# Delta rule: a dense product in the turns of the last unit, whose result is not read

## The chip, the cores and the metric

The kernel runs as one program on one core of a Trainium2 chip. TensorE (PE) multiplies matrices, VectorE (DVE), ScalarE (ACT) and GpSimd (POOL) work on elements, and DMA queues move data between memories. The metric is the device time of one execution in microseconds. TensorE's clock is granted by the chip: the profile writes 1.00 for 2.4 GHz and 0.50 for 1.2 GHz.

## The reference

Four transformer layers with modulated layer norms are computed in float32. The change touches the attention part of the last one, a gated delta rule over 8 sequences of 512 positions with 8 heads, keys of 128 and values of 32 elements:

```python
def step(state, inp):
    q_t, k_t, v_t, a_t, b_t = inp
    retained = jnp.einsum('bhvk,bhk->bhv', state, k_t)
    rk = retained[..., None] * k_t[:, :, None, :]
    vk = v_t[..., None] * k_t[:, :, None, :]
    state = a4 * (state - b4 * rk) + b4 * vk
    return (state, jnp.einsum('bhvk,bhk->bhv', state, q_t))
q = _l2norm(_causal_dw_conv_silu(x @ Wq, conv_q).reshape(bsz, seq_len, H, KD))
...
out = out * rms * o_norm_w * jax.nn.silu(gate)
return out.reshape(bsz, seq_len, VAL_DIM) @ Wo
```

k and v are made like q (v without the norm). After it comes one more part, the channel mix, and the store of the result.

## The kernel before

`delta_rule` cuts the work into 16 units: unit u is sequence u // 2 and one half of its heads (four). A unit has four chunks of 128 positions (NT = 4), and a chunk takes nine turns (NI = 9), so a unit takes TU = 36 turns. Within a chunk the step by step recurrence is replaced by a triangular system. Its inverse is built in blocks of 32 in the turns of `invert`: X and Y are the inverse and its transpose, F a product between them; each turn issues sixteen products of 32x32 on PE (L2194), and DVE or ACT takes the result. One chunk later, in the turns of `solve`, the system is solved: turn 0 applies the state to queries and keys (L2225, not for a unit's first chunk), turns 1, 3, 5, 7 apply the inverse (L2237) and turns 2, 4, 6 the blocks before (L2230), with DVE between each and the next; turn 8 makes the output and the new state (L2243, L2247). `make` prepares the next chunk: L2179 in turn 0 spreads the decays, L2187 in turns 3 and 6 multiplies keys with queries and keys with keys (four products of 128x128).

Around these stands a list of pieces with a turn and a place each (`pieces_at`), which `in_turn` walks in the same order on every engine. Turns of a later unit's preparation lie in the turns of the unit before: the projections of queries and keys ("taps", L2281 and L2285, five products of 128x512 to each chunk of nine turns, in turns 8, 0, 1, 2 and 3, into banks P[4] and P[5]), the sums of squares (L2293), values and gates (L2270, L2271), transposed keys (L2311). An engine issues its instructions in that order, and semaphores hold it until its inputs are there. The last unit, u = 15, has no unit behind it to prepare: after its own projections are done, at 15 turns ahead of its turn 0, P[4] and P[5] are no longer written, and its own 36 turns and the nine of the last `solve` run with what belongs to it alone. Then the unit's results are scaled (`rms`), transposed (L2319) and multiplied with Wo3 (L2324), and DVE adds them to X (L2620), which ends the stage. The channel mix begins with L2654.

In the page and the trace a float32 matmul shows as two records, so that four products are x8.

```python
if 0 <= turn < NU * TU:
    invert(u, i, *INVERT[step])
for piece in at.get((turn, 2), ()):
    prepare(*piece)
```

These four lines close a turn in `in_turn`; a piece without a place of its own has place 2, and so stands behind the turn's `solve` and `invert`.

Of the kernel before, what the change touches and what calls it, by code (L numbers as in the profile page):

```python
# [24 lines left out]
T = 512  # L25
# [88 lines left out]
def ts(i, n):  # L114
    return slice(i * n, (i + 1) * n)
# [1869 lines left out]
def delta_rule(k):  # L1985
# [3 lines left out]
    with ExitStack() as s:  # L1989
# [4 lines left out]
        hp_of = lambda u: hp2[:, u // 2 % 2]  # L1994
# [22 lines left out]
        pe, act, dve, pool, dma = k.stage("delta_start")  # L2017
# [20 lines left out]
        for n in (1,):  # L2038
            pe, act, dve, pool, dma = k.stage(f"delta_taps{n}")
# [23 lines left out]
        NI = len(INVERT)  # L2063
        NU, TU = 2 * B, NT * NI

        def pieces_at():

            at = {}  # L2070

            def put(u, turn, *piece, place=2):
                at.setdefault((TU * u + turn, place), []).append((u,) + piece)

            for turn in range(-6 * NI, NU * TU, NI):
                put(0, turn - 1, "table", 0)
            for u in range(NU):
                if u % 2 == 0:
                    for turn, x in ((-55, 1), (-54, 2), (-52, 3)):
                        put(u, turn, "norm", x)  # L2080
                for turn, piece in ((-36, ("small", 0)), (-35, ("gate", 0)), (-33, ("gate", 1)), (-30, ("gate", 2)), (-24, ("gate", 3)), (-24, ("gate", 4))):
                    put(u, turn, *piece)
                for x in range(5):
                    put(u, x - 9, "norms", x)
                for x in range(32):
                    turn = NI * (x // 8) - 50 + x % 8
                    if x % 8 == 0:
                        put(u, turn - 1, "taps", x)
                    elif x % 8 >= 4:
                        put(u, turn, "taps", x, place={8: 0, 0: 0, 1: 1}.get(turn % NI, 2))  # L2090
                for x in range(0, 8, 2):
                    for j in range(TAPS):
                        put(u, NI * (x // 2) - 50 + (0, 0, 1, 3)[j], "conv", TAPS * x + j, place=(1 if j == 0 else 2))
                for x in range(8):
                    put(u, NI * (x // 2) - 46 + 4 * (x % 2), "taps_done", x, place=(1 if x % 2 == 0 else 2))
                    put(u, NI * (x // 2) - 42 + 2 * (x % 2), "squares", x)
                for x in range(NT):
                    put(u, NI * x - 14, "values", x)
                    put(u, NI * x - 13, "values_done", x)
                    put(u, NI * x - 3, "scale", x)  # L2100
                put(u, 16, "weigh", 0)
                for x in range(NT - 1):
                    put(u, NI * x - 11, "keys", x)
                    put(u, NI * x - 10, "keys_done", x)
                for turn, x in ((9, 0), (11, 1), (12, 2), (13, 3)):
                    put(u, TU + turn, "rms", x)
                if u % 2:
                    for turn, x in ((14, 0), (15, 1), (16, 2)):
                        put(u, TU + turn, "out", x)
            return at  # L2110

        def all_units(name):
# [39 lines left out]
            tap_bank = lambda run: P[4 + run % 2]  # L2152
# [15 lines left out]
            with nc.Block() as block:  # L2168
                @block.tensor
                def _(e):  # L2170
# [79 lines left out]
                    def prepare(u, what, x):  # L2250
                        tag, g = f"u{u}", u % 2
# [14 lines left out]
                        elif what == "values":  # L2266
                            emptied(e, u, "values", x)
                            cols, b = ts(g, 128), ring_bank(u, "values", x)
                            for j in range(TAPS):
                                e.matmul(b[:, 0:128], hp_of(u)[:, j + x * C:j + x * C + C], w_v[:, j, cols], start=(j == 0), stop=(j == TAPS - 1))  # L2270
                            e.matmul(b[:, 128:256], hp_of(u)[:, 3 + x * C:3 + x * C + C], k.w["Wg3"][:, cols], start=True,  # L2271
                                     stop=True).then_inc(pe.steps, pe.did(f"{tag}values{x}"))
                        elif what == "taps":
                            run, j = x // 4, x % 4
                            c, H, b = run % 2, 4 * g + run // 2, tap_bank(run)
                            if c == 0:
                                if x == 0:
                                    e.wait_ge(dve.steps, dve.at(f"u{u - g}nh"))
                                if u or run:
                                    e.wait_ge(dve.steps, dve.at(f"{tag}conv{TAPS * run - 5}" if run else f"u{u - 1}conv27"))  # L2280
                                e.matmul(b, w_q[:, ts(H, C)], hp_of(u)[:, 3:3 + T], start=True, stop=True).then_inc(pe.steps, pe.did(f"{tag}run{run}"))  # L2281
                                return
                            if j == 0 and (u or run > 1):
                                e.wait_ge(act.steps, act.at(f"{tag}run{run - 2}" if run > 1 else f"u{u - 1}run{run + 6}"))
                            ins = e.matmul(b, w_k[:, j, ts(H, C)], hp_of(u)[:, j:j + T], start=(j == 0), stop=(j == TAPS - 1))  # L2285
                            if j == TAPS - 1:
                                ins.then_inc(pe.steps, pe.did(f"{tag}run{run}"))
                        elif what == "squares":
                            e.wait_ge(pool.steps, pool.at(f"{tag}sq{x}"))
                            if x == 0 and u:  # L2290
                                e.wait_ge(dve.steps, dve.at(f"u{u - 1}ssq"))
                            row = 4 * (x % 2) + x // 2
                            e.matmul(few[0:8, :], k.w["picks"][:, row, :], squares(x), start=(x == 0), stop=(x == 7)).then_inc(pe.steps, pe.did(f"{tag}ss{x}"))  # L2293
                        elif what == "norms" and x == 1:
                            e.wait_ge(dve.steps, dve.at(tag + "rows"))
                            for i in range(NT):
                                ins = e.matmul(few[:, ts(i, 8)], sq_rows[:, ts(i, C)], k.w["ident"][0:8, 0:8], start=True, stop=True)
                            ins.then_inc(pe.steps, pe.did(tag + "ssq"))
                        elif what == "gate" and x == 2:
                            hs = ts(g, 4)  # L2300
                            e.wait_ge(dve.steps, dve.at(tag + "g"))
                            emptied(e, u, "gate", 2)
                            b = ring_bank(u, "gate", 2)
                            e.matmul(b[:, 0:16], k.w["upto3"][:], q["g"][:, :, hs], start=True, stop=True)
                            e.matmul(b[:, 16:32], k.w["ones3"][:], q["g"][:, :, hs], start=True, stop=True).then_inc(pe.steps, pe.did(tag + "cum"))
                        elif what == "keys":
                            emptied(e, u, "keys", x)
                            e.wait_ge(act.steps, act.at(tag + "run7"))
                            b = ring_bank(u, "keys", x)
                            for h in range(4):  # L2310
                                ins = e.transpose(b[:, ts(h, C)], QK[:, 1, 4 * (u % 3) + h, ts(x, C)], k.w["ident"][:])  # L2311
                            ins.then_inc(pe.steps, pe.did(f"{tag}keys{x}"))
                        elif what == "out":
                            emptied(e, u, "out", x)
                            b = ring_bank(u, "out", x)
                            if x < 2:
                                e.wait_ge(dve.steps, dve.at(tag + "normed"))
                                for i in range(NT):
                                    ins = e.transpose(b[:, ts(i, C)], O[:, i, ts(x, 4)].rearrange("p h x -> p (h x)"), k.w["ident"][:])  # L2319
                                ins.then_inc(pe.steps, pe.did(f"{tag}oT{x}"))  # L2320
                            else:
                                e.wait_ge(act.steps, act.at(f"{tag}oT1"))
                                for half in range(2):
                                    ins = e.matmul(b, k.w["Wo3"][:, half, :], OT[:, half], start=(half == 0), stop=(half == 1))  # L2324
                                ins.then_inc(pe.steps, pe.did(tag + "att"))
# [584 lines left out]
```

## Time and profile before

| what | value |
|---|---|
| median of 3 runs | 3779.19 us (3778.6 to 3787.32) |
| the profiled execution | 3768.31 us |
| its span | 3766.5 us |
| PE busy in the span | 3335.2 us, 89% |
| DVE, ACT, POOL busy | 2340.3, 1697.2, 529.5 us |
| mean granted clock | 0.916 |

The span is the time between the first and the last instruction in the trace, and the execution's own time is a little longer. The last unit's turns lie near 3584 to 3678 us of the span, the channel mix behind 3693. All positions in the trace below are us from the span's start.

### The profile page before, as it was taken

How to read it: one execution, taken by the hardware profiler on the slowest of the kernel's cores; microseconds unless marked ns; L12 is line 12 of the kernel's file. 1: busy time of each engine (PE TensorE's matmuls, PEld its weight loads, DVE VectorE, ACT ScalarE, POOL GpSimd, SP SyncE). 2: the span in 40 equal slices, each digit the busy share in tenths (PEclk: the TensorE clock that was granted, in tenths of full speed). 3: DMA queues.
4: the chain of work that ended last, by engine and by line, in shares of the span. 5: the costliest groups of instructions: out<-in, count | busy, mean ns of one | idle time of the engine just before them, and what ended most of it. 6: DMA issues, size and time to landing. Idle time of an engine off the chain costs nothing. (4 is left out here: it accounts for less than half of the span.)

```text
span 3766.5 us, 124901 instructions
## 1 busy us (share of the span) xinstructions
PE 3335.2 (89%) x55256; PEld 2060.0 (55%) x55256; DVE 2340.3 (62%) x6284; ACT 1697.2 (45%) x3930; POOL 529.5 (14%) x533
## 2 busy tenths in 40 slices
PE   5878876789999999999999859999999999999985
PEld 2337743345555555555555326666666666666772
DVE  5758853487776767777773125666665666666545
ACT  3659963554444544443322434444444444343323
POOL 1214420000000000000000002222222222222211
PEclk9989987898998989889888979999999999999967
DMA  2000001211111111110000010000000000000000
GB/s 95 0 20 2 2 1 46 78 45 42 42 48 36 47 39 45 42 42 31 3 3 3 0 47 2 2 3 3 2 3 3 3 2 3 3 2 3 3 2 25
DMA packets 37035, 77.16 MB, mean 20 GB/s; under 512 B 7696, under 2 KB 11152, under 8 KB 35472
## 3 DMA queue, kind: packets, MB, share of 16 engines
q1 hardware_dynamic: 36496, 69.17, 5.6%
q8 instruction: 437, 7.16, 0.8%
q14 instruction: 102, 0.84, 0.1%
HBM read 64.83 MB, written 4.33 MB: 18 GB/s over the span
## 5 line engine op out<-in xcount | busy, mean ns | idle before, releaser
L1608 ACT ACTIVATE g_hidden<-ps 128x512 f32<-128x512 f32 x224 | 133.1, 594 | 398.6 <-PE ps L1466 398.6
L1466 PE MATMUL ps<-w_w 128*128 128x512 f32 x448 | 268.7, 684 | 44.5 <-DVE w_w L1816 28.8
L1322 PEld LDWEIGHTS ps<-g_Q,g_K 32*32 32x32 f32 x12288 | 190.2, 112 | 187.2 <-issue 125.2
L2285 PE MATMUL ps<-d_hp,d_w_k 128*128 128x512 f32 x512 | 281.3, 636 | 0.0
L2363 POOL TENSOR_TENSOR d_sq<-d_QK 128x512 f32<-128x512 f32 x128 | 133.0, 1039 | 864.6 <-ACT d_QK L2414 702.7
L1482 PE MATMUL ps<-g_hidden,w_w 128*128 128x512 f32 x448 | 254.5, 655 | 0.0
L2383 ACT ACTIVATE d_F<-ps 128x128 f32<-128x128 f32 x256 | 70.8, 276 | 348.9 <-PE ps L2194 345.7
L1322 PE MATMUL ps<-g_Q,g_K 32*32 32x32 f32 (+1 forms) x12288 | 220.6, 216 | 6.4 <-issue 4.4
L795 ACT ACTIVATE att_p<-ps,att_mx 128x96 f32<-128x96 f32 x512 | 175.4, 518 | 6.0 <-DVE att_mx L736 6.0
L1290 POOL COPY g_xb<-X 128x512 f32<-128x512 f32 x8 | 7.2, 906 | 1183.8 <-DVE X L1828 1083.6
L2558 DVE SCALAR_TENSOR_TENSOR d_conv<-ps,w_conv_q,d_conv 128x511 f32<-128x511 f32 (+2 forms) x192 | 142.2, 741 | 33.9 <-ACT d_conv L2408 30.0
L2341 POOL TENSOR_TENSOR d_M<-d_A,w_joins 128x128 f32<-128x128 f32 (+1 forms) x128 | 114.3, 912 | 345.5 <-ACT d_A L2377 345.5
L2194 PE MATMUL ps<-d_X,d_M 32*32 32x32 f32 x8192 | 123.8, 196 | 41.4 <-DVE d_X L2490 21.6
L795 ACT ACTIVATION_READ_ACCUMULATOR att_p<-ps,att_mx 128x1 f32 x512 | 156.8, 386 | 0.0
L1634 DVE TENSOR_TENSOR g_S<-g_S,ps 128x128 f32<-128x128 f32 x64 | 18.4, 288 | 221.2 <-PE ps L1338 221.1
L2187 PE MATMUL ps<-d_QK 128*128 128x128 f32 x1024 | 154.5, 296 | 0.0
L2517 DVE TENSOR_TENSOR d_r<-d_r,ps 32x128 f32<-32x128 f32 x192 | 55.0, 286 | 160.1 <-PE ps L2230 89.0
L2194 PEld LDWEIGHTS ps<-d_X,d_M 32*32 32x32 f32 x8192 | 96.2, 108 | 101.5 <-issue 65.9
L2377 ACT ACTIVATE d_A<-d_A 32x128 f32<-32x128 f32 x256 | 78.6, 307 | 158.2 <-DVE d_A L2478 153.5
L1338 PEld LDWEIGHTS ps<-g_V,g_KT 32*32 32x32 f32 x4096 | 74.7, 112 | 135.3 <-issue 107.0
L2373 ACT ACTIVATE d_D<-d_D 128x512 f32<-128x512 f32 x64 | 40.3, 629 | 235.9 <-DVE d_D L2465 235.9
L1610 ACT ACTIVATE g_hidden<-g_hidden 128x512 f32<-128x512 f32 x224 | 141.1, 630 | 7.1
(504 smaller groups left out, 7894.0 us busy)
## 6 DMA issues: line engine op xcount, KB each, us to landing
w_w<-gate_rows SPq DMA_DIRECT2D x56, 256.0 KB, 3.4
w_w<-in_c_fc_dram SPq DMA_DIRECT2D x56, 256.0 KB, 4.1
w_w<-in_c_proj_dram SPq DMA_DIRECT2D x56, 256.0 KB, 2.7
X<-in_x_dram SPq DMA_DIRECT2D x1, 2048.0 KB, 8.3
w_c_fc<-in_c_fc_dram SPq DMA_DIRECT2D x1, 2048.0 KB, 12.7
w_c_proj<-in_c_proj_dram SPq DMA_DIRECT2D x1, 2048.0 KB, 17.1
ex_root<-gate_rows SPq DMA_DIRECT2D x1, 2048.0 KB, 13.8
h_rows<-k SPq DMA_DIRECT2D x1, 2048.0 KB, 6.3
```

What stands on the lines that cost most here:

```text
L795: e.activation(p[:, n % 2, i, 0:NK], scored[:, g, b], ACT.Exp, bias=mx[:, n % 2, i:i + 1], accum_out=den[:, n % 2, i:i + 1]).then_inc(act. ...
L1322: ins = e.matmul(later(scored, n_), keys_, queries(n_, planes, r_, 4 * i + j), start=(turn_ == 0 and part == 0 and n_ != 1), stop=(part == 1),
L1466: e.matmul(P[2], fc[:, n % 2, ts(f, C)], hs[n % 2], start=True, stop=True).then_inc(pe.steps, pe.did(now(f"u{i}")))
L1482: e.matmul(P[3], proj[:, n % 2, f, :], r[:, (16 * c["half"] + i) % 5], start=(c["half"] == 0 and i == 0), stop=(c["half"] == 1 and i == 15 ...
L1608: e.activation(r[:, slot], P[2], ACT.Relu).then_inc(act.steps, act.did(now(f"r{i}")))
L1610: e.activation(r[:, slot], r[:, slot], ACT.Square).then_inc(act.steps, act.did(now(f"q{i}")))
L2187: ins = e.matmul(mk[:, ts(h, C)], QK[:, 1, H, t], QK[:, part - 1, H, t], start=True, stop=True)
L2194: ins = e.matmul(inv[rows, h], stationary[rows, h], moving[rows, h], start=True, stop=True, tile_position=(32 * j, 32 * j))
L2285: ins = e.matmul(b, w_k[:, j, ts(H, C)], hp_of(u)[:, j:j + T], start=(j == 0), stop=(j == TAPS - 1))
L2341: e.tensor_tensor(M[:, a, levels], A32[:, a].unsqueeze(1).to_broadcast([C, many, 4, 32]), k.w["joins"][:, levels].unsqueeze(2).to_broadcas ...
L2363: e.tensor_tensor(squares(x), qk, qk, ALU.mult).then_inc(pool.steps, pool.did(f"{tag}sq{x}"))
L2558: e.scalar_tensor_tensor(cv[:, late:], tap_bank(run)[:, 0:T - late], k.w["conv_q"][:, 4 * g + run // 2, 3 - late:4 - late], cv[:, late:], ...
```

## The change

In the last unit, each turn from 1 to 43 whose number within the chunk is neither 0 nor 8 gets one more product on PE: the identity times the unit's 128x512 normalised input, into bank P[4]. That is seven in each of five runs of turns (1 to 7, 10 to 16, 19 to 25, 28 to 34, 37 to 43), 35 in all. It stands at place 2, the end of the turn. Nothing reads the result and nothing waits for it; it has no semaphore step of its own. It waits for the last reads of P[4] by ACT and DVE.

```diff
+                if u == NU - 1:
+                    for turn in range(1, TU + NI - 1):
+                        if turn % NI not in (0, NI - 1):
+                            put(u, turn, "dense", turn)
             return at
...
+                        elif what == "dense":
+                            e.wait_ge(act.steps, act.at(f"{tag}run7"))
+                            e.wait_ge(dve.steps, dve.at(f"{tag}conv{4 * 6 + 3}"))
+                            e.matmul(tap_bank(0), k.w["ident"][:], hp_of(u)[:, 3:3 + T], start=True, stop=True)
                         elif what == "out":
```

## Rows read from the trace of the kernel before

**Rows 1.** The page's slices of the span: the granted clock in tenths, 40 slices.

```profile
PEclk9989987898998989889888979999999999999967
```

**Rows 2.** Windows of all engines: the last unit's stretches, and an ordinary chunk (last row).

```profile
core 0: us, PE busy (x) PEld busy (x) DVE busy (x) ACT busy (x) POOL busy (x), PEclk, DMA share, GB/s
3588.53:3601.86 13.33, 11.37 (x312) 9.88 (x311) 7.77 (x24) 4.42 (x11) 1.28 (x2) 0.75 0.02 4
3601.86:3604.81 2.95, 2.54 (x48) 2.27 (x48) 1.08 (x5) 2.09 (x3) 1.66 (x2) 1.00 0.00 0
3604.81:3618.04 13.23, 10.16 (x308) 8.85 (x307) 10.10 (x29) 5.04 (x14) 2.60 (x3) 0.87 0.01 2
3618.04:3626.85 8.81, 8.81 (x73) 8.39 (x73) 1.90 (x8) 1.19 (x1) 2.70 (x3) 0.55 0.01 2
3626.85:3640.93 14.08, 11.93 (x298) 10.49 (x297) 8.07 (x25) 3.08 (x10) 1.62 (x2) 0.50 0.01 2
3640.93:3650.13 9.20, 7.83 (x64) 7.52 (x65) 2.04 (x10) 1.17 (x1) 1.48 (x2) 0.50 0.01 2
3650.13:3658.99 8.86, 8.01 (x280) 6.89 (x280) 4.96 (x18) 1.11 (x4) 0.00 (x0) 0.50 0.02 5
...
3668.20:3675.57 7.37, 4.40 (x56) 3.46 (x56) 2.30 (x8) 0.00 (x0) 0.00 (x0) 0.50 0.01 2
3675.57:3688.20 12.63, 7.20 (x20) 4.53 (x20) 3.11 (x7) 1.63 (x4) 1.04 (x1) 0.54 0.00 0
3434.24:3456.31 22.07, 20.16 (x393) 14.30 (x392) 14.52 (x44) 8.36 (x20) 7.34 (x7) 1.00 0.01 3
```

**Rows 3.** Timeline of PE: start, length, line, operation, idle time before it.

```profile
3428.82 1.02 PE L2285 MATMUL ps<-d_hp,d_w_k 128*128 128x512 f32 x2
3429.68 0.97 PE L2243 MATMUL ps<-d_zz,d_P 128*128 128x32 f32 x8
...
3436.24 1.12 PE L2285 MATMUL ps<-d_hp,d_w_k 128*128 128x512 f32 x2
3437.30 0.43 PE L2237 MATMUL ps<-d_r,d_Y 32*32 32x32 f32 x8
3437.66 1.16 PE L2187 MATMUL ps<-d_QK 128*128 128x128 f32 x8
3438.75 0.45 PE L2194 MATMUL ps<-d_X,d_M 32*32 32x32 f32 x32
3439.13 1.12 PE L2281 MATMUL ps<-d_hp,d_w_q 128*128 128x512 f32 x2
...
3540.45 1.87 PE L2225 MATMUL ps<-d_S,d_QK 128*128 128x32 f32 x16
...
3606.74 0.45 PE L2194 MATMUL ps<-d_X,d_M 32*32 32x32 f32 x32 [1.49 <-DVE d_X L2487]
...
3645.45 3.62 PE L2225 MATMUL ps<-d_S,d_QK 128*128 128x32 f32 x16 [0.32 <-DVE d_O L2540]
...
3696.54 2.07 PE L2658 MATMUL ps<-c_tmp,w_mean 128*128 128x512 f32 x2 [0.69 <-ACT c_tmp L2689]
3698.41 1.91 PE L2654 MATMUL ps<-X,w_center 128*128 128x512 f32 x2
```

**Rows 4.** Windows counting L2187 alone: window, length, PE and PEld busy, granted clock.

```profile
3553.80:3560.50 6.70, 1.16 (x8) 0.97 (x8) 1.00 0.01 2
3571.20:3574.50 3.30, 2.08 (x8) 1.78 (x8) 0.50 0.00 0
3577.30:3584.50 7.20, 1.16 (x8) 0.97 (x8) 1.00 0.01 2
...
3614.30:3618.50 4.20, 1.16 (x8) 0.97 (x8) 1.00 0.02 4
3619.50:3680.00 60.50, 4.15 (x16) 3.56 (x16) 0.50 0.01 2
```

## The prediction

> **What bounds the kernel now.** I went from coarse to fine. The page's slices show TensorE's granted clock near full all through the delta rule and falling in the last slices before the channel mix [rows 1]. Next I cut the last unit's turns into stretches at the instructions that open and close them [rows 2]: the seven turns 1 to 7 of a chunk (into which the change puts its products), and the stretch of turns 8 and 0 between them (which gets none). These stretches follow one another without a gap from 3588.53 to 3675.57; their lengths are 13.33, 2.95, 13.23, 8.81, 14.08, 9.20, 8.86, 9.21 (a second one like the 9.20, not shown) and 7.37, together 87.0 us, and then 12.6 us to the end of the stage. Three things are to be seen. PE is busy for 80 to 100% of each, so PE's own instruction order sets the end. The level is mixed up to 3618 and 1.2 GHz (0.50) from there on. And an ordinary chunk of the unit before, which has projection products of 512 columns among its turns, holds 2.4 GHz (1.00) through all of its 22.07 us.
>
> The prize is what the low level costs. The state products (L2225) take 1.87 us at 2.4 GHz and 3.62 at 1.2 [rows 3]. The price is PE time: the engine runs its matmuls in order, and the new product stands ahead of the next turn's.
>
> What goes with the clock is read from the group of windows that count only L2187 (eight records are four products of 128 columns, 512 columns in all) [rows 4]. The level held to 3560.5 with the last such group begun at 3553.8, to 3584.5 with one at 3577.3, and only to about 3618.5 with one at 3614.3: it fell some 3 to 6 us after the end of the last wide group. It came back 3.3 us after a group had begun. Over the 60.5 us from 3619.5 the level stayed at 1.2 GHz with two such groups, although PE was busy for 48.8 of the 57.5 us of the six stretches from 3618 on [rows 2], mostly with 32-column products. So the wide products go with the level, not the time for which PE is occupied.
>
> **The change, part by part.** It removes and moves nothing. It adds 35 products of 128x512, seven in each of the last unit's five runs of turns 1 to 7. Their two waits (run7 on ACT, conv27 on DVE) belong to the unit's projections, whose last pieces stand 15 and more turns ahead of its turn 0, so they hold nothing; were one held, L2237 and L2230 of the next turn would wait behind it on PE, and DVE for them. Nobody reads their bank, and nobody waits for them; only PE is touched. No DMA is added.
>
> *Price of one product at 2.4 GHz.* L2285 has this shape. From its start to the start of the L2237 behind it, with no idle time between, it is 1.06 us (3436.24 to 3437.30); the smallest such distance is 0.86, with an L2243 behind it (3428.82 to 3429.68) [rows 3]. The bounds for 35 are 30 and 37 us. I take 1.06, since L2237 or L2230 stands behind nearly all new products. At 1.2 GHz the distance is 1.87 (3696.54 to 3698.41).
>
> *What covers it.* Idle PE time in the seven-turn stretches is 1.96, 3.07, 2.15, 0.85 and 2.97 us (length less busy). Of the first three about 1.5 us each is the wait for the first X of the chunk, which comes ahead of the first new product (1.49 in the row of L2194, [rows 3]) and stays. The rest, some 6 us, is cover. That is far less than the 37 us: most of the product time lies on the path.
>
> *Stretches with the products, if the level is 2.4 GHz.* Distances at that level: L2237 0.36, L2194 0.38, L2187 1.09 [rows 3]; L2230 about 0.38, since its own wait for DVE passes behind a product.
> - Run 1: 13.33 before. 7 x 1.06 = 7.4 is added; the level is 1.2 GHz until about 3595, so nearly two products cost 0.8 more each (+1.4); cover takes 0.5; the L2187 group and what followed it at the low level now falls after the rise (-1.7). About 19.9.
> - Run 2: 13.23 + 7.4 - 1.6 of cover - 1.2 for the low piece around 3610 that goes. About 17.9.
> - Run 3: seven times (0.37 + 0.38 + 1.06), two L2187 groups of 1.09, and 1.5 of wait: 16.4, against 14.08.
> - Run 4: seven times 1.81, 12.7, against 8.86.
> - Run 5 (solve alone): seven times (0.37 + 1.06), 10.0, against 7.37.
> - Between them: 2.95 unchanged; 8.81 becomes 5.8 and 9.20 and 9.21 become 5.6 each (busy time times 0.53, which is 1.16 to 2.08 and nearly 1.87 to 3.62, plus idle time that DVE's part of the chain leaves).
> Sum 19.9 + 2.95 + 17.9 + 5.8 + 16.4 + 5.6 + 12.7 + 5.6 + 10.0 = 96.9, against 87.0: +10. In the 12.6 us behind, PE is busy for 7.20 at a level of 0.54: all at 2.4 GHz would save 3.4, L2243's part of it about 0.9. I take -2, since the level may fall again in the idle time ahead of the transposes. So **+8 us even if the level never falls**.
>
> *What the stretches without products do.* From the end of a run's last product to the first product of the next run there are 8.0 us at turn 17 (5.8, then 0.36, about 1.5 of wait and 0.38), 6.4 at turn 26 and 6.0 at turn 35. The level fell 3 to 6 us after the last wide group [rows 4], so I expect it to fall in each of the three, at about 5 us, and to come back some 4.5 us after the next product begins (3.3 was seen, but a fall may come just before). The first stretch then has 3.0 us of its work at the low level, +2.5; the others 1.0 to 1.4, +0.8 each. In the 4.5 us of low level in the run a turn takes 2.96 us, not 1.81, which costs 4.5 x 0.39 = 1.75, three times. Together +9, so **+17 us**. Ends: fall at 6 and return after 2.5 gives +4 (sum +12), fall at 3.5 and return after 7 gives +17 (sum +25). The stretch of turns 8 and 9 is not counted: only 5.3 us lie between its products, with an L2179 group of 512 columns among them.
>
> The Trainium skill, "TensorE: Matmul & The Clock Gate", section "Why this matters for your kernels", says to keep TensorE busy with no idle gap over about 3 us, else its clock drops. The trace disagrees in part: with PE busy 85% of the time and no idle time over 1.5 us the level stayed at 0.50 [rows 2, 3]. By that rule the level would not fall in the stretches without products, since PE has matmuls there, and the sum would be +8 and not +17.
>
> **Rivals.**
> 1. *The level holds across the turns without products.* For it: it held for at least 5.5 and 6.0 us behind wide groups twice [rows 4]. Against: it fell after 3 once, and the stretch at turn 17 is over 8. Price: the +8 above, 3787 us. The Trainium skill's rule above would come out here.
> 2. *A faster end.* The products cost next to nothing, because they run beside PE's waits and beside small products on other parts of the array. Then only the level counts: -3.0, -3.6, -3.6 between runs, -3.1, -1.9 and -1.6 in runs 3 to 5, -2 in runs 1 and 2, -2 behind: -21 us, 3758. It decides from the point where a product takes less than 1.06 - 8/35 = 0.83 us of the chain (rival 1's level) or 0.57 (mine). Against: the smallest distance is 0.86, and the run's idle time is 6 us beyond the fixed waits.
> 3. *The level never returns* once down, one product per turn being too little. 35 x 1.87 less 6 of cover, and run 1 and 2 lose 7 us of high level: +66, 3845. Against: the ordinary chunk holds 1.00 with five projection products of 512 columns and two of squares in its nine turns.
> 4. *Longer falls than I took*: return after two or three turns each time, +25 to +35, 3804 to 3814.
>
> **How the numbers follow.** The profiled execution took 3768.3 us (span 3766.5), 0.3% under the median of the runs, 3779.2. I add the difference to both: 3785 in a profile, and 3779.2 + 17 = 3796 as the median. Chances: my forecast 0.59, rival 1 0.24, rival 2 0.04, rival 3 0.03, rival 4 0.10. The range runs from a rival 1 with products a little cheaper (+3) to rival 4's upper part (+32): 3782 to 3811; the forecast's own is 3791 to 3804. A measurement of this kernel tells about 0.3%, 11 us, from no change. Faster by more than that is rival 2 alone, 0.04. Within it lies rival 1 and the low tail of mine, 0.27. Slower: 0.69.
>
> **What would show it.** In the profile after: 35 products (70 records) at the new line, 1.06 us apart from what follows at 1.00 and 1.87 at 0.50; PE without idle time in turns 2 to 7; the level 1.00 in most of each run, with a low piece that begins in the second half of each stretch without products and ends within two turns of the next run; runs of about 20, 18, 18, 14 and 12 us; DVE's waits for PE longer in the same turns; everything before 3588 as it was. The prediction is wrong if a product's distance is well under 1.06 (then too high), if the level holds or never holds in the stretches without products, or if executions differ in where the level falls, which a shift of a few us would do.

## The result, and the profile after

The changed kernel took 3796.7 us (median of 15 runs, 3789.0 to 3808.7) against 3776.7 us for the kernel before in the same comparison (15 runs): ratio 1.0053, 95% interval 1.0040 to 1.0067, so 15 to 25 us slower. Its profiled execution took 3802.0 us with a span of 3799.0.

The page of the changed kernel: the row of busy times, and the granted clock in 40 slices.

```profile
PE 3375.9 (89%) x55326; PEld 2066.0 (54%) x55326; DVE 2339.4 (62%) x6284; ACT 1698.2 (45%) x3930; POOL 529.6 (14%) x533
...
PEclk9889987889888989889887979999999999999887
```

PE has 70 records more, the 35 products. The last three slices read 8, 8, 7 where they read 9, 6, 7 [rows 1]; the second of them holds most of the last unit. The level there is higher, and the time longer.

The windows of all engines in the last unit, cut as before at turn 1 of each chunk and at the first L2247 (before: L2243) behind each run; columns as in [rows 2].

```profile
3599.01:3620.74 21.73, 20.44 (x326) 12.71 (x326) 7.78 (x24) 5.55 (x12) 2.44 (x3) 0.73 0.01 2
3620.74:3623.50 2.76, 2.44 (x49) 2.16 (x47) 1.00 (x5) 0.96 (x2) 0.65 (x1) 1.00 0.00 0
3623.50:3640.67 17.17, 15.68 (x322) 9.66 (x321) 10.12 (x29) 5.51 (x14) 3.07 (x4) 1.00 0.01 3
3640.67:3647.24 6.57, 6.37 (x73) 6.00 (x72) 1.83 (x8) 0.73 (x1) 2.29 (x2) 0.81 0.00 0
3647.24:3665.82 18.58, 17.29 (x311) 9.68 (x310) 8.20 (x25) 3.52 (x10) 2.07 (x3) 0.79 0.01 2
3665.82:3673.38 7.56, 5.99 (x66) 5.73 (x65) 2.04 (x10) 0.73 (x1) 1.07 (x1) 0.69 0.01 2
3673.38:3687.97 14.59, 14.44 (x295) 7.70 (x296) 4.96 (x18) 1.11 (x4) 0.00 (x0) 0.81 0.02 4
3687.97:3693.76 5.79, 4.22 (x65) 3.98 (x65) 1.89 (x8) 0.00 (x0) 0.00 (x0) 0.90 0.00 0
3693.76:3707.61 13.85, 13.85 (x70) 6.02 (x71) 2.30 (x8) 0.00 (x0) 0.00 (x0) 0.67 0.00 1
3707.61:3720.10 12.49, 6.67 (x21) 3.61 (x20) 3.48 (x7) 1.62 (x4) 1.04 (x1) 0.59 0.00 0
```

The five runs take 21.7, 17.2, 18.6, 14.6 and 13.9 us, against 13.3, 13.2, 14.1, 8.9 and 7.4 [rows 2]. The three stretches between the later runs take 6.6, 7.6 and 5.8, against 8.8, 9.2 and 9.2. From turn 1 to turn 44 it is 108.6 us, against 87.0: +21.6. Up to the start of DVE's last add, which ends the stage, it is then 11.7 us (3707.61 to 3719.33) against 12.3 (3675.57 to 3687.82): half a microsecond is given back. (The windows shown end a little later, and not at the same point of that add in both.) PE, which had 1 to 3 us of idle time in each run, is now idle for 0 to 1.5.

PE's timeline, two places: start, length, operation, idle time before.

```profile
3627.62 1.12 PE L2320 MATMUL ps<-d_hp,w_ident 128*128 128x512 f32 x2
3628.67 0.43 PE L2241 MATMUL ps<-d_r,d_Y 32*32 32x32 f32 x8
...
3649.17 0.66 PE L2198 MATMUL ps<-d_X,d_M 32*32 32x32 f32 x32 [1.29 <-DVE d_X L2495]
3649.75 2.08 PE L2320 MATMUL ps<-d_hp,w_ident 128*128 128x512 f32 x2
3651.76 0.64 PE L2234 MATMUL ps<-d_W,d_A 128*32 128x32 f32 x8
```

At 2.4 GHz the next operation starts 1.05 us after the product (3627.62 to 3628.67; 1.06 at 3638.00, not shown), as L2285 had it [rows 3]; at 1.2 GHz 2.01 us (3649.75 to 3651.76). The first product of a run stands behind the wait for X.

The level, and the records of L2320 in each piece (window, length, PE busy, PEld busy, granted clock).

```profile
3594.00:3610.00 16.00, 4.33 (x5) 1.18 (x6) 0.50 0.01 2
3611.00:3644.40 33.40, 12.42 (x23) 3.29 (x22) 1.00 0.01 2
3645.00:3654.40 9.40, 3.57 (x4) 1.00 (x4) 0.50 0.01 2
3655.00:3668.40 13.40, 5.63 (x10) 1.49 (x10) 1.00 0.01 2
3669.00:3678.40 9.40, 2.62 (x3) 1.00 (x4) 0.50 0.01 3
3679.00:3692.40 13.40, 6.12 (x12) 1.49 (x10) 1.00 0.01 2
3693.00:3702.40 9.40, 6.62 (x7) 1.90 (x8) 0.50 0.00 0
```

This is the shape that was forecast. Read in windows of 0.1 us, the level falls at 3644.8, 3668.7 and 3692.6, each time in a stretch without products and 2.7 to 4.5 us after the end of the last one. It returns at 3655.0, 3678.9 and 3702.8, which is 5.3, 4.2 and 8.5 us after the first product of the next run began (3649.75, 3674.71, 3694.30). The three low pieces are equally long, 10.2 us each; how much of one lies among products depends on where it begins. The piece at the start, up to 3610.6, is 5 us longer, counted from turn 1, than it was in the kernel before (11.6 us against 6.5, to 3595.1). It ended only 9.1 us after the first new product (3601.51).

### The profile page after: what moved, and what is told of

Read it like the earlier page. It is cut to its first block and busy times, and to the rows that moved or that the text cites. A ratio compares the mean times of both kernels' runs of the same rounds, so it can differ in the third digit from the quotient of the medians.

```text
span 3799.0 us, 125076 instructions
## 1 busy us (share of the span) xinstructions
PE 3375.9 (89%) x55326; PEld 2066.0 (54%) x55326; DVE 2339.4 (62%) x6284; ACT 1698.2 (45%) x3930; POOL 529.6 (14%) x533
## 6 DMA issues: line engine op xcount, KB each, us to landing
ex_root<-gate_rows SPq DMA_DIRECT2D x1, 2048.0 KB, 13.9
```

## The experiments

All have the arithmetic of the kernel before for the output; only products whose result is not read differ. Each ratio is to the kernel before on the same chip. The executions of one kernel scatter by half a per cent and more, so beside each ratio stands the length from turn 1 to turn 44 in its profile, which is read to a few hundredths of a microsecond but belongs to one execution.

**gaps_filled**

```diff
-                        if turn % NI not in (0, NI - 1):
+                        if turn % NI not in (0, NI - 1) or turn in (8, 17, 18, 26, 27, 35, 36):
```

> The 35 products stay and seven more stand in turns 8, 17, 18, 26, 27, 35 and 36, so that no stretch of the last unit is without 512-column products for long. My theory (about half of the loss is product time on PE, the other half is that the level falls in the stretches without products and comes back late): granted clock 1.00 from the first rise to turn 44, the stretches between runs 6 to 7.5 us with the products in them, runs 3, 4 and 5 at 16.4, 12.7 and 10.0 us; from turn 1 to turn 44 about 100 us against the 108.6 of the changed kernel, and a median some 8 us under it, near +12 us to the kernel before. Rival (falls cost nothing, all of the loss is product time): seven more products add 4 to 7 us, +25 us.

Measured: ratio 1.0023 (0.9997 to 1.0049), +9 us; turn 1 to 44 in 97.0 us. Windows of the stretch at turn 17 and all behind it, to turn 44:

```profile
3640.20:3647.08 6.88, 6.88 (x78) 5.56 (x77) 2.49 (x11) 0.72 (x1) 2.29 (x2) 1.00 0.00 0
3647.08:3662.28 15.20, 14.56 (x311) 8.53 (x311) 7.45 (x23) 3.52 (x10) 2.08 (x3) 1.00 0.01 3
3662.28:3668.45 6.17, 6.06 (x69) 4.69 (x69) 2.04 (x10) 0.73 (x1) 1.07 (x1) 1.00 0.00 0
3668.45:3680.99 12.54, 12.20 (x295) 6.59 (x295) 4.85 (x18) 1.11 (x4) 0.00 (x0) 1.00 0.02 5
3680.99:3687.05 6.06, 5.95 (x69) 4.58 (x69) 1.90 (x8) 0.00 (x0) 0.00 (x0) 1.00 0.00 0
3687.05:3696.89 9.84, 9.84 (x71) 4.51 (x71) 2.30 (x8) 0.00 (x0) 0.00 (x0) 1.00 0.01 2
```

The level is 1.00 in every row. With six of the seven added products in them (the seventh is in turn 8), these six stretches take 56.7 us, against 66.9 in the changed kernel. The rival (falls cost nothing) asked for +25 us, above the interval (its upper end is +18), and is out. The three runs took 15.2, 12.5 and 9.8 us, close to the 16.4, 12.7 and 10.0 worked out for them.

**small_product**

```diff
-                            e.matmul(tap_bank(0), k.w["ident"][:], hp_of(u)[:, 3:3 + T], start=True, stop=True)
+                            e.matmul(tap_bank(0)[:, 0:8], k.w["ident"][:], hp_of(u)[:, 3:3 + 8], start=True, stop=True)
```

> The same 35 instructions with 8 columns instead of 512. My theory: each costs about 0.1 to 0.15 us of PE, hidden in part, +1 to +4 us, and the level behaves as in the kernel before, 1.2 GHz from about turn 16 on. Rival (the loss comes from having the instructions, their waits and weight loads in the order, and not from the columns streamed): +15 us or more.

Measured: ratio 1.0042 (1.0022 to 1.0063), +16 us; turn 1 to 44 in 100.6 us. First its windows of run 3, the stretch behind it and run 4, then one product and what follows on PE:

```profile
3633.43:3650.49 17.06, 15.54 (x312) 14.05 (x311) 8.22 (x25) 3.39 (x10) 1.97 (x3) 0.50 0.01 3
3650.49:3659.69 9.20, 7.83 (x64) 7.52 (x65) 2.04 (x10) 0.86 (x1) 1.07 (x1) 0.50 0.00 0
3659.69:3671.27 11.58, 11.34 (x295) 10.36 (x295) 4.97 (x18) 1.11 (x4) 0.00 (x0) 0.50 0.01 4
```

```profile
3637.62 0.59 PE L2320 MATMUL ps<-d_hp,w_ident 128*128 128x8 f32 x2
3638.14 0.63 PE L2241 MATMUL ps<-d_r,d_Y 32*32 32x32 f32 x8
```

The level behaved as expected: mixed in runs 1 and 2 (0.64 and 0.65), then 0.50 in every stretch from run 3 on. The price did not: an 8-column product takes 0.52 us of PE at 1.2 GHz (3637.62 to 3638.14) and 0.32 at 2.4 (3600.42 to 3600.74), not 0.1 to 0.15. Run 3 went from 14.08 to 17.06 and run 4 from 8.86 to 11.58. 35 times 0.52 is 18; PE's idle time in the five runs fell by 5.7 us (11.0 to 5.3), and that leaves 12.5 of the +13.6 seen. So my expectation for this run (+1 to +4) was wrong by more than three times, and the rival's number came out. The trace also says which part of the rival: the order and the waits cost nothing (the product starts without idle time before it), but its two weight loads take 0.50 us at 1.2 GHz and 0.30 at 2.4, nearly the whole distance:

```profile
3637.61 0.50 PEld L2320 LDWEIGHTS ps<-d_hp,w_ident 128*128 128x128 f32 x2
...
3600.42 0.30 PEld L2320 LDWEIGHTS ps<-d_hp,w_ident 128*128 128x128 f32 x2
```

Beside a full product's 1.06 us, the 0.32 of the small one is about a third that hardly goes with the columns.

**runs_1_2**

```diff
-                    for turn in range(1, TU + NI - 1):
+                    for turn in range(1, 2 * NI):
```

> Only the 14 products of turns 1 to 7 and 10 to 16, where the level was mostly high before. My theory: pure cost there, run 1 +6 to +8 us and run 2 +4 to +5, a gain of up to 2 in the stretch behind, then runs 3 to 5 at 1.2 GHz as before: +9 to +11 us. Rival (the products pay by the level they give): 0 or faster.

Measured: ratio 1.0010 (0.9987 to 1.0034), which tells nothing apart; turn 1 to 44 in 93.2 us, +6.2. Windows of runs 1 and 2, the stretch behind run 2, and run 3:

```profile
3576.56:3595.90 19.34, 18.05 (x325) 11.34 (x325) 7.78 (x24) 5.55 (x12) 2.43 (x3) 0.84 0.01 3
3598.67:3618.46 19.79, 18.30 (x321) 10.71 (x321) 10.12 (x29) 5.51 (x14) 3.07 (x4) 0.83 0.01 2
3618.46:3624.04 5.58, 5.30 (x74) 4.99 (x73) 1.78 (x9) 0.73 (x1) 2.30 (x2) 1.00 0.01 3
3624.04:3636.22 12.18, 9.14 (x297) 7.79 (x297) 8.04 (x26) 3.06 (x10) 1.61 (x2) 0.86 0.02 4
```

Runs 1 and 2 cost 6.0 and 6.6 us more than before. The stretch behind gives 3.2 back and run 3 1.9; the stretch after it another 1.1. The two runs together cost what was expected (run 2 alone more than its +4 to +5: the level fell once more inside it, from 3599.9 to 3606.7), but the return was 6 us and not 2, so that +6.2 stands where I had +9 to +11. Only the 3.2 of the stretch behind, where the level is now 1.00, can be put down to the products: in before_again below, run 3 and the stretch after it took 12.51 and 8.91 us without any.

**waits_only**

```diff
-                    for turn in range(1, TU + NI - 1):
-                        if turn % NI not in (0, NI - 1):
-                            put(u, turn, "dense", turn)
+                    for turn, place in ((1, 1), (10, 1), (19, 1), (27, 2), (36, 2), (31, 2)):
+                        put(u, turn, "dense", turn, place=place)
+                    for c in range(NT):
+                        put(u, NI * c + 7, "dense", NI * c + 7)
+                        put(u, NI * c + 8, "dense", NI * c + 8)
```

> 14 products, each where PE waited before: turns 7 and 8 at the end of each chunk, between L2237 and the first L2194 in turns 1, 10 and 19, at the end of turns 27 and 36, and one in turn 31; none in the last run. My theory: a product costs only what its 1.06 us exceeds the wait it stands in (0.5 to 1.5 us), 6 to 8 us in all, and keeps the level at 2.4 GHz up to the last run, which gives back about 3 us each in three stretches and 2 to 3.5 in runs 3 and 4: 8 to 14 us faster than the kernel before. Rival (products cannot be hidden, or the level falls anyway with so few): no change or up to 14 x 1.06 = 15 us slower.

Measured: ratio 0.9986 (0.9964 to 1.0007), -5 us with the interval touching 1; turn 1 to 44 in 76.9 us, 10.1 less than before. The run alone is inconclusive by its median. Its windows of run 3, of run 4, and from turn 44 to the end of the stage:

```profile
3634.44:3645.30 10.86, 9.78 (x300) 7.12 (x300) 8.04 (x26) 3.06 (x10) 1.60 (x2) 1.00 0.01 3
3651.47:3661.17 9.70, 8.89 (x285) 5.76 (x285) 4.85 (x18) 1.11 (x4) 0.00 (x0) 0.82 0.02 4
3673.66:3687.00 13.34, 7.60 (x20) 4.52 (x20) 3.41 (x7) 1.63 (x4) 1.04 (x1) 0.50 0.00 0
```

The length is what the theory asked for, the level only in part: it is 1.00 in runs 2 and 3 and in every stretch between runs, but 0.68 in run 1 (15.5 us, 2.2 more than before) and it falls in run 4, from 3654.4 to 3657.8.

**before_again**, the kernel before without an edit.

> The kernel before, unchanged, as a measure of what differs from execution to execution. My theory of the last unit (its length is set by PE's order and by where the level falls): 87 us from turn 1 to turn 44 in the first profile, here between 82 and 92, since only the place of the falls and returns may shift; ratio to itself within 0.3%. Rival (the differences between kernels in the last unit are of the size of such shifts): this length moves by 10 us or more.

Measured: ratio 1.0006 (0.9986 to 1.0025); turn 1 to 44 in 88.2 us. Its windows of run 1 and run 3:

```profile
3582.62:3597.21 14.59, 12.66 (x312) 11.16 (x311) 7.77 (x24) 4.42 (x11) 1.27 (x2) 0.66 0.01 2
3623.95:3636.46 12.51, 9.45 (x298) 8.17 (x297) 8.06 (x25) 3.06 (x10) 1.60 (x2) 0.76 0.01 3
```

The level fell and returned at other places: run 1 took 14.59 us at 0.66 (before: 13.33 at 0.75), run 3 12.51 at 0.76 (14.08 at 0.50). Single stretches move by up to 1.6 us, the whole by 1.2. The differences in the whole length told here are 6 to 22 us; a difference of 1 or 2 us in one stretch is not told apart from this.

**no_tail**

```diff
-                    for turn in range(1, TU + NI - 1):
+                    for turn in range(1, TU):
```

> The changed kernel without the seven products of the last run (turns 37 to 43). My theory: that run goes from 13.85 us to between 5.8 (2.4 GHz) and 7.4 (1.2 GHz), the rest stays near 94.8: turn 1 to 44 in 101 us, about +13 to +14 us to the kernel before. Rival (what the level gives to the last run and to the products behind it pays for them): no gain by leaving them out.

Measured: turn 1 to 44 in 100.6 us, 8 less than the changed kernel, with the last run at 7.38 us and 0.50. Of these 8 us, 6.5 lie in the last run (13.85 to 7.38), the rest ahead of it in the same code. The ratio, 1.0058 (1.0035 to 1.0081), +22 us, doesn't show this gain: its interval reaches down to +13 us, where the expectation lay, but its middle is no lower than the changed kernel's +20. The gain stands on one profile alone.

The same code of runs 1 and 2 stands in the changed kernel, here and in runs_1_2, and it did not run alike. In the changed kernel's profile the level was 1.00 through run 2, which took 17.2 us. Here it fell in it, from 3612.2 to 3615.6, and run 2 took 18.5; in runs_1_2 it took 19.8.

**waits_end**

```diff
-                    for turn, place in ((1, 1), (10, 1), (19, 1), (27, 2), (36, 2), (31, 2)):
+                    for turn, place in (..., (45, 2), (46, 2), (47, 2)):
```

> The 14 products in PE's waits, and three more in turns 45 to 47, where PE stood idle for 4.2 us ahead of the last unit's transposes. My theory: turn 1 to 44 near 77 us as with the 14 alone; the stretch from turn 44 to the end of the stage goes from 12.6 to about 10 us, since the transposes (1.94 us) and the output product (3.34) run at 2.4 GHz: 12 to 13 us faster than the kernel before. Rival (the level there does not come up in time): the end as with the 14 alone, 12.6 us.

(The line with a minus is that of waits_only.) Measured: ratio 0.9955 (0.9936 to 0.9974), -17 us; turn 1 to 44 in 74.8. The profile is of the slowest of its 12 executions (3779.7 us; the median is 3759.4), so it speaks for the last unit and not for the whole time. The window from turn 44 to the end of the stage:

```profile
3688.70:3699.40 10.70, 9.17 (x26) 4.94 (x26) 3.39 (x7) 1.52 (x4) 1.04 (x1) 0.77 0.00 0
```

10.7 us at a level of 0.77, where the run with the 14 alone had 13.3 at 0.50 over the same work: 2.6 gained from products that stand in idle time. The transposes take 1.06 us there, against 1.94.

**waits_wide**

```diff
-                    for turn, place in ((1, 1), (10, 1), ...):
+                    for turn, place in ((-8, 1), (1, 1), (10, 1), ...):
...
-                    for c in range(NT):
+                    for c in range(-2, NT):
```

> As the run with the three products at the end, and five more in the waits of the unit before, after the last projection: turns -11, -10, -8, -2 and -1 as counted from the last unit's turn 0. The level fell there too in the kernel before (1.2 GHz from about 3561 to 3574.5 and from 3585 to 3595). My theory: those 23 us of low level go, which gives back 6 to 9 us for about 2 us of price, and the first run begins at 2.4 GHz: 16 to 21 us faster than the kernel before. Rival (the five cost what they give back): 12 us faster, as without them.

(The lines with a minus are those of waits_end.) Measured: ratio 0.9950 (0.9932 to 0.9968), -19 us by the ratio and 3755.1 us as the median: faster than the kernel before, and the fastest kernel of this study by its number, though its interval overlaps that of the run before it. Turn 1 to 44 in 72.8 us. The last unit, cut as above, and then what stands at its end on PE:

```profile
3589.46:3601.42 11.96, 11.27 (x314) 8.90 (x315) 7.54 (x24) 4.96 (x12) 1.83 (x3) 1.00 0.01 3
3601.42:3604.65 3.23, 3.23 (x51) 2.54 (x49) 1.00 (x5) 1.55 (x2) 1.10 (x1) 1.00 0.02 5
3604.65:3617.42 12.77, 10.97 (x311) 8.26 (x311) 10.10 (x29) 5.04 (x14) 2.60 (x3) 1.00 0.02 4
3617.42:3623.59 6.17, 6.09 (x75) 5.36 (x75) 1.78 (x9) 1.19 (x1) 2.70 (x3) 1.00 0.00 0
3623.59:3634.45 10.86, 9.79 (x300) 7.13 (x300) 8.03 (x26) 3.05 (x10) 1.60 (x2) 1.00 0.02 5
3634.45:3640.62 6.17, 6.06 (x69) 4.69 (x69) 2.04 (x10) 1.20 (x1) 1.48 (x2) 1.00 0.00 0
3640.62:3648.98 8.36, 7.54 (x285) 5.20 (x285) 4.85 (x18) 1.11 (x4) 0.00 (x0) 1.00 0.02 5
3648.98:3655.12 6.14, 6.03 (x69) 4.66 (x69) 1.89 (x8) 0.00 (x0) 0.00 (x0) 1.00 0.01 3
3655.12:3662.31 7.19, 4.20 (x57) 3.29 (x57) 2.30 (x8) 0.00 (x0) 0.00 (x0) 0.56 0.00 0
3662.31:3674.00 11.69, 10.11 (x26) 5.39 (x26) 3.43 (x7) 1.51 (x4) 1.04 (x1) 0.69 0.00 0
```

```profile
3664.03 5.47 PE L2322 MATMUL ps<-d_hp,w_ident 128*128 128x512 f32 x6
3669.29 1.18 PE L2329 MATMUL ps<-w_ident,d_O 128*128 128x128 f32 x8
```

The level is 1.00 in eight stretches, from turn 1 to turn 36, and falls only in the last run, which has no products, at 3655.9 and so 0.9 us after the end of the last product. There the three products of turns 45 to 47 began at 1.2 GHz and took 5.3 us (3664.03 to 3669.29), more than the 4.2 us of idle time: they pay less here than in the run before. In the unit ahead the gain is seen between the copies that open the first solve of one unit and of the next: 86.3 us in the kernel before (3517.6 to 3603.9), 88.2 in waits_end, and 82.2 here, with a level of 0.96 against 0.86 and 0.85. (In before_again, the same code as before, it is 87.7.) By the profile the rival (they cost what they give) falls; by the two ratios it doesn't.

## Why the prediction was right

**The sum.** Forecast +17 us, measured +20 (15 to 25). Up to turn 44 it was put at +19 (96.9 and 9, less 87.0) and came out at +21.6 in the profile. The median was put at 3796 and was 3796.7; this close hit is partly luck, since the difference was 3 us short and the kernel before 2.5 us quicker than in its first three runs. The forecast execution was 3785 us in a profile; it was 3802. Of these 17 us, 10.5 lie ahead of turn 1 (which begins at 3599.01 and not at 3588.53), in code that is the same; no experiment was made on that. In before_again turn 1 began 5.9 us earlier than before, so such shifts come with the execution.

**Price of a product.** 1.06 us was forecast from L2285 and 1.05 to 1.06 measured. At 1.2 GHz it was 2.01 and not 1.87. That a third of the 1.06 hardly goes with the columns was not in the forecast and did not enter its sum.

**Cover.** Some 6 us was right in kind: PE's idle time in the runs fell from 11.0 to 4.2 us (the first waits for X stayed). The prediction says that PE was busy for 80 to 100% of each stretch; by its own rows it is 60% in run 5 (4.40 of 7.37 us) and 77% in run 2. The sums don't use that reading, since they take the idle time stretch by stretch.

**Stretches at 2.4 GHz.** Runs 3 to 5 and the stretches between them were put at 56.1 us; gaps_filled, which holds the level, took 56.7 with six products more in them. By stretches that were at 2.4 GHz without products (5.58 us in runs_1_2, 5.90 and 5.79 in no_tail, against 6.88, 6.17 and 6.06 with two products each), these six cost about 1.9 us, so that 54.8 is an estimate without them: the forecast had these stretches 1.3 us too long. Run 2 was put at 17.9 and took 17.2, but 18.5 and 19.8 in no_tail and runs_1_2, where the level fell at its start. The prediction counted no fall for the stretch of turns 8 and 9; in the changed kernel's profile that held, but in those two the level fell just behind that stretch, before the first product of run 2.

**Falls.** Three were forecast, in the three stretches without products, and three came. Their price was put at +9: the changed kernel took 66.9 us where 56.1 were worked out, +10.8, and against the 54.8 above it is +12. So this term was short by 2 to 3 us, and the too long stretches hid part of it. The last fall was the dearest, since the level came back 8.5 us after the first product and not 4.5, so that run 5 took 13.9 us and not 11.8. The first run was short too: 21.7 us and not 19.9, since the level came back only at 3610.6. In the three other kernels with products of 512 columns in all its turns it took 19.3 to 19.9, so this may be a matter of the execution. The -2 behind turn 44 was too much: the level fell again in the idle time ahead of the transposes, and half a microsecond came.

**The rivals.** That the level holds across the stretches is refuted by the profile and by gaps_filled. That the products cost nothing is refuted by the distance of 1.06. But the part of rival 2 that lies in PE's waits is real, and I gave it no place of its own: products put *only* there made the kernel faster (waits_end, waits_wide). That the level never returns is refuted. Longer falls than the forecast's (rival 4) came once in three: the last low piece reached into the fourth of the seven turns of run 5. The Trainium skill ("TensorE: Matmul & The Clock Gate", "Why this matters for your kernels") asks for no idle gap over about 3 us; here the level fell with PE busy for 6.4 of 6.6 us, so by this trace the rule is not enough: a PE without idle gaps did not keep the level where the wide products were missing.

Left open: whether leaving out the last run's products is worth its 8 us in the median, how waits_end and waits_wide stand to each other, and what sets the moment of a fall or a return, which differs between executions of the same code. That the products in PE's waits pay by the level, and not by standing there, was not tested with small ones in the same places. Each length and level here is from one profiled execution of its kernel.

## What to carry to other kernels

A product issued only to keep TensorE's clock was paid nearly in full here wherever PE was already the bound, so count its distance to the next instruction against what the low level costs in the same turn: 1.06 us for each was more than the level gave back here, and the same products in PE's waits were less (half a per cent of the whole time gained, with 17 and 22 of them). Look first where PE waits or stands idle (ahead of a DVE result, ahead of a transpose), put one there and none elsewhere, and see that no stretch is left long without wide work, because each fall of the changed kernel reached from such a stretch into the next run.

## What the runs showed of the hardware

- A product of 8 columns with a 128x128 weight takes 0.32 us of PE at 2.4 GHz and 0.52 at 1.2, in float32, of which its weight loads are 0.30 and 0.50; one of 512 columns takes 1.06 and 2.01.
- 35 products of 8 columns, in the same turns as the wide ones, did not raise the level: it stayed at 0.50 through runs 3 and 4, with PE busy for 15.5 of 17.1 and 11.3 of 11.6 us.
- Fourteen wide products in the waits held 2.4 GHz in runs 2 and 3 as 42 in nearly all turns did: 1.00 in run 3 in both, with 10.9 against 15.2 us. In run 4 the fourteen had a fall (0.82) where the 42 had none.
- In the changed kernel the level came back 9.1, 5.3, 4.2 and 8.5 us after the start of the first new product at 1.2 GHz, and fell 2.7 to 4.5 us after the end of the last one ahead of each stretch without products. The spread over the kernels is wider: back 2.0 us after the product in waits_only (3655.76 to 3657.8), and down 0.9 us after it in waits_wide (3655.0 to 3655.9).
